# The second block's residual in one flat transfer beside the shifted values, and new order words: a two-stage sequence kernel on one core

## What is computed

```
x = x + _layernorm(_L0_attn_ref(_layernorm(x, axis=-1), ...), axis=-1)
x = x + _layernorm(_L0_ffn_ref(_layernorm(x, axis=-1), ...), axis=-1)
```

```
da = jnp.exp(dt_t[:, :, None] * a)
dbu = dt_t[:, :, None] * b_t[:, None, :] * u_t[:, :, None]
state = da * state + dbu
y_t = jnp.einsum('bds,bs->bd', state, c_t)
```

## Time and profile before

| | us |
|---|---|
| median of 3 runs | 2424.35 |
| lowest and highest run | 2414.93, 2427.51 |
| the profiled execution | 2425.17 |
| its span, first to last instruction | 2423.4 |
| one sequence in the steady state | 136.93 to 139.19 |
| PE, DVE, ACT, POOL busy in the span | 1934.9, 1914.2, 1741.6, 1716.1 |
| the four loads of the residual, each | 64 KB, 2.7 to landing |

### The profile page before, as it was taken

How to read it: one execution, slowest core, us unless ns; L and a number is a source line. 1 busy time by engine, 2 the same in 40 slices (tenths; PEclk the granted TensorE clock), 3 DMA queues, 4 the chain that set the end, 5 groups by cost and what they waited for, 6 DMA issues and landing times.

```text
span 2423.4 us, 43963 instructions
## 1 busy us (share of the span) xinstructions
PE 1934.9 (80%) x15823; PEld 1138.6 (47%) x15936; DVE 1914.2 (79%) x3509; ACT 1741.6 (72%) x3891; POOL 1716.1 (71%) x1572
## 2 busy tenths in 40 slices
PE   2255889798988979797988979797988979788866
PEld 0012446363635446363645546363644536364634
DVE  3557797979889797988888797988889797987442
ACT  2245778696978778696877879696877869686644
POOL 1959596877959596886959596895959597792110
PEclk9967999998999999899999989999999999899988
DMA  5444343535345453535434353534434353541000
GB/s 167 126 114 119 107 119 96 131 101 145 100 118 131 107 123 89 142 82 151 113 110 122 108 125 95 142 91 132 124 105 119 106 133 94 140 104 34 17 16 14
DMA packets 126346, 261.09 MB, mean 108 GB/s; under 512 B 26928, under 2 KB 59696, under 8 KB 125872
## 3 DMA queue, kind: packets, MB, share of 16 engines
q1 hardware_dynamic: 126128, 258.27, 40.4%
HBM read 185.42 MB, written 42.99 MB: 94 GB/s over the span
## 4 chain that ended last, share of the span: by engine, by line
PE 37%; ACT 18%; DVE 18%; POOL 14%; issue 10%; DMA 2%; SPq 0%; POOLq 0%; DVEq 0%; ACTq 0%
POOL dbu L663 5%; POOL gy L680 5%; ACT late L893 4%; DVE m L928 4%; PE b_bank L357 3%; PE f_bank L357 3%; ACT da L609 3%; DVE kr L942 3%; PE b_bank L763 2%; POOL kr L997 2%; PE y_sum L584 2%; PE b_bank L780 2%; PE b_bank L746 2%; PE f_bank L746 2%; PE f_bank L763 2%
## 5 line engine op out<-in xcount | busy, mean ns | idle before, releaser
L629 DVE TENSOR_TENSOR_SCAN hs<-da,dbu 128x512 f32<-128x512 f32 x512 | 623.3, 1217 | 112.5 <-POOL dbu L663 67.6
L680 POOL TENSOR_TENSOR gy<-hs,bc 128x512 f32<-128x512 f32 x512 | 652.7, 1275 | 34.2 <-DVE hs L629 21.8
L663 POOL TENSOR_TENSOR dbu<-spread,bc 128x512 f32<-128x512 f32 x512 | 652.2, 1274 | 16.5 <-DMA spread<-steps 16.5
L609 ACT ACTIVATE da<-spread,rest 128x512 f32<-128x512 f32 x512 | 362.3, 708 | 140.2 <-DVE hs L629 121.1
L720 PE MATMUL b_bank<-rest,h_t 128*128 128x512 f32 x384 | 245.8, 743 | 75.4 <-DVE kr L942 71.5
L997 POOL TENSOR_TENSOR kr<-kr,rn 128x512 f32<-128x512 f32 x256 | 261.0, 1044 | 32.9 <-ACT rn L853 18.4
L720 PE MATMUL f_bank<-rest,h_t 128*128 128x512 f32 x384 | 235.8, 717 | 40.2 <-DVE kr L942 30.4
L584 PE MATMUL y_sum<-gy,rest 128*32 128x512 f32 x1024 | 146.4, 647 | 93.3 <-POOL gy L680 93.3
L357 PE MATMUL b_bank<-first,kr 128*128 128x128 f32 x768 | 127.5, 291 | 82.3 <-DVE kr L942 60.4
L893 ACT ACTIVATE late<-b_bank,mx 128x128 f32<-128x128 f32 x512 | 141.0, 383 | 60.5 <-DVE mx L958 60.5
L1146 POOL TENSOR_TENSOR xs<-xs,v 128x512 f32<-128x512 f32 x16 | 18.9, 1183 | 215.9 <-ACT xs L352 215.9
(11 more groups left out here) (171 smaller groups left out, 4789.3 us busy)
## 6 DMA issues: line engine op xcount, KB each, us to landing
spread<-steps SPq DMA_DIRECT2D x256, 512.0 KB, 4.7
vs<-v SPq DMA_DIRECT2D x96, 260.0 KB, 5.6
steps<-k_t SPq DMA_DIRECT2D x32, 512.0 KB, 3.0
bc<-bc_rows SPq DMA_DIRECT2D x32, 512.0 KB, 6.4
gate<-gates SPq DMA_DIRECT2D x32, 512.0 KB, 5.4
gates<-kr SPq DMA_DIRECT2D x16, 512.0 KB, 2.9
gates<-late SPq DMA_DIRECT2D x16, 512.0 KB, 3.9
vs<-v SPq DMA_DIRECT2D x32, 130.0 KB, 4.7
```

Source lines behind the costliest of these rows:

```text
L609: e.activation(da[:, :], spread[:, slot(b, s // 2), 0, :], ACT.Exp, scale=a_neg[:, s:s + 1]).then_inc(decayed.sem, 1)
L629: e.tensor_tensor_scan(hs[:, s % 2, :], da[:, :], dbu[:, s % 2, :], 0.0, ALU.mult, ALU.add).then_inc(scanned.sem, 1)
L663: e.tensor_tensor(dbu[:, s % 2, :], spread[:, slot(b, s // 2), 1, :], bc[:, s % 2, :], ALU.mult).then_inc(fed.sem, 1)
L680: e.tensor_tensor(gy[:, s % 8, :], hs[:, s % 2, :], bc[:, 2 + s % 2, :], ALU.mult).then_inc(read_out.sem, 1)
```

## The change

- `residual` moves from `wb.v` to `wb.vs[:, 0]`, taken flat as 512 numbers in a row. It lies over the shifted values of the first block, zeroed half included.
- `x1_rows` is laid out by partition (4, P, T) instead of by position, so that the store of x1 and the load of the residual move 2 KB in a row for each partition, and the load is one DMA instead of four. The add on POOL reads flat.
- The wait for `o_made(b - 1)` goes from ACT's first value copy to SP, ahead of the first shifted copy (`sp_windows`, i = 0).
- All five order words are new.

```diff
-        residual = wb.v[:, :, 0:2, 0:DH]
+        residual = wb.vs[:, 0, :, :].rearrange("p h d -> p (h d)")[:, 0:T]
...
-            e.dma_start(x1_rows[b % 4, :, :].rearrange("(t p) d -> p t d", p=P), x1[:, :, :]).then_inc(x1_stored.sem, 16)
+            e.dma_start(x1_rows[b % 4, :, :], x1[:, :, :].rearrange("p t d -> p (t d)")).then_inc(x1_stored.sem, 16)
...
         def sp_windows(E, e, b, w):
             for i in range(2):
+                if i == 0 and w is wb and b > 0:
+                    E.wait_ge(*o_made(b - 1))
                 E.wait_ge(*w.v_copied(b, 2 * i + 1))
...
                 E.wait_ge(*w.projected(b, projections.index(take)))
-                if w is wb and b > 0 and t == 0:
-                    E.wait_ge(*o_made(b - 1))
                 e.activation(w.v[:, t, :, 0:DH], heads(bank_of(take)[:, :]), ACT.Copy).then_inc(w.v_copied.sem, 1)
...
-            x = xs[b % 3][:, :, :].rearrange("p t (g d) -> p t g d", g=2)
+            x = xs[b % 3][:, :, :].rearrange("p t d -> p (t d)")
             E.wait_ge(*o_normed(b))
-            E.wait_ge(*x1_loaded(b, NT - 1))
+            E.wait_ge(*x1_loaded(b))
...
-            for t in range(NT):
-                e.dma_start(residual[:, t, :, :], x1_rows[b % 4, t * P:(t + 1) * P, :].rearrange("p (g d) -> p g d", g=2)).then_inc(
-                    x1_loaded.sem, 16)
+            e.dma_start(residual, x1_rows[b % 4, :, :]).then_inc(x1_loaded.sem, 16)
```

One of the words, SP's, with its delays:

```diff
-        "M3 A1 M8 S2 B1 M1 C1 S1 F2 M9 B1 A1 B1 M1 E1",
-        "A5 B10 C5 E0 F2 M34 S3"),
+        "M4 A1 M4 B2 E1 M1 C1 M2 A1 M3 B1 M5 F1 S2 M1 S1 F1 M2",
+        "A8 B15 C6 E2 F4 M64 S6"),
```

More of the change, by code:

```diff
@@ L43 @@
     "pe": (
[4 rows of a table removed]
[4 rows of a table added]
     "act": (
[5 rows of a table removed]
-    "dve": (
[5 rows of a table removed]
[5 rows of a table added]
+    "dve": (
[5 rows of a table added]
     "pool": (
-        "M5 A1 M1 A2 M12 E1 M31 F4 C1 B2 M1 A1 M3 A1 B1 A1 B1 M4 A1 B2 M2 A2 B1 M3 B2 M2 A1 M3 B3 A2",
-        "A27 B36 C4 E1 F4 M116"),
+        "M3 F4 C1 B1 A1 B1 A2 M2 B1 M2 B1 M1 B1 M2 B1 M1 A1 M2 A1 M1 B1 M1 A1 M2 B1 M1 B1 M2 A1 M1 B3 M1 A1 M2 A1 "
+        "M4 A1 M1 A2 M2 E1 M36",
+        "A24 B36 C4 E0 F4 M70"),
     "sp": (
-        "M3 A1 M8 S2 B1 M1 C1 S1 F2 M9 B1 A1 B1 M1 E1",
-        "A5 B10 C5 E0 F2 M34 S3"),
+        "M4 A1 M4 B2 E1 M1 C1 M2 A1 M3 B1 M5 F1 S2 M1 S1 F1 M2",
+        "A8 B15 C6 E2 F4 M64 S6"),
 }
@@ L269, in build @@
         steps, bc_rows = dram("steps", (2, DI, 2, T)), dram("bc_rows", (2, 2 * NS, T))
-        gates, x1_rows = dram("gates", (2, DI, 2, T)), dram("x1_rows", (4, T, D))
+        gates, x1_rows = dram("gates", (2, DI, 2, T)), dram("x1_rows", (4, P, T))
         x_loaded, e_normed = sig("x_loaded", 1, 16), sig("e_normed", 1)
@@ L293, in build @@
                                                  sig("x2_made", 1))
-        x1_loaded, o_normed, o_made, stored = sig("x1_loaded", NT, 16), sig("o_normed", 1), sig("o_made", 1), sig("stored", 1, 16)
+        x1_loaded, o_normed, o_made, stored = sig("x1_loaded", 1, 16), sig("o_normed", 1), sig("o_made", 1), sig("stored", 1, 16)
         w_loaded, rest_loaded, tables_loaded = sig("w_loaded", 1, 16), sig("rest_loaded", 1, 16), sig("tables_loaded", 1, 16)
```

## The result

| | before | after |
|---|---|---|
| median, us (4 runs each, same chip) | 2419.64 | 2459.68 |
| lowest and highest | 2414.73, 2427.51 | 2457.97, 2459.90 |
| span of the profiled execution | 2423.4 | 2457.9 |

The ratio is 1.016, with a 95% interval of 1.0131 to 1.0188. The forecast was 2420 with a range up to 2444.

The account below looks back on a forecast made before the run. No engine is full, so the period of 137.5 us between residual adds decides. 12.5 periods x -0.5 = -6, plus 2 at the ends, from a profiled 2425.2 lying 0.8 above the median: 2420 us, range 2402 to 2444.

Parts of the forecast that it names:

- The wait off ACT: First value copy's 13.1 us wait for POOL's residual add goes, but ACT's next wait, for POOL's clip, stays: 0.
- The residual's transfer: One load instead of four on SP: the freed 3 us a period stand where nobody waits, 0 to +0.7, taken 0.
- 0.3 to 0.7 us: Cover left before group 12 is read, with the residual's load now ahead of it; POOL would not wait at scan 24.
- The stores: SP's new store order lands the first group about 4 us later, covered by front work: 0 to +2.5, taken 0.
- That leaves 0.5 to 1.5 us: Cover between the first group's later landing and ACT's first da and POOL's first dbu.
- rival (1): Stores pile up beyond the cover, first group 3 us later: +1.8 a period, 2443 us; chance 0.17.
- POOL's work is only exchanged ... By the second and third scan both orders have done the same work: At the first scan, POOL's wait of 0.67 us for the root becomes about 0.8 for the sum of squares.
- rival (2): Reordering shifts PE's pauses and clock: long periods go, 2411, or all become long, 2437; chance of the latter 0.06.
- a mean clock in a period that moves by 0.02: Sign that PE's clock, through the new order, had changed the length of the periods.
- The second step size product: In the entry, later by 1.9 us, of which POOL's work order gives back some 0.6: +1.3.
- The handover: To the next sequence: clip of dt off the chain ahead of `xs`, -0.3 to -0.6 us a period, taken -0.5.
- The ends: First sequence has no cover for du and the loads landing later; last back layer runs alone: +2 us in total.

Follow-up runs that it names:

- code_alone: The changed kernel's code under the five old order words, against the kernel before: 2423.94 us, ratio 0.9992.
- spill_first: The changed kernel with SP storing z, u, x1, b and c ahead of dt and du: 2450.24 us, 1.0106 of the kernel before.
- start_back: spill_first with POOL, ACT and DVE in the old order at the first scan: 2449.62 us, 1.0129 of the kernel before.
- busy_after: The changed kernel with four added products on PE ahead of the back layer's K1 turn: 2444.89 us, 1.0101 of the kernel before.
- busy_more: The kernel before with eight added products in PE's pauses: 2410.56 us, 0.9964 of the kernel before.
- dt_back: spill_first with eight of 24 products of the back layer's last projection behind the second step size product again: 2448.30 us, 1.0118 of the kernel before.
- entry_part: New code, old order, except PE, ACT and DVE in the new order from state norm to handover: 2422.46 us, 1.0015 of the kernel before.
- busy_spill: spill_first plus four added products on PE ahead of the back layer's K1 turn: 2432.00 us, 1.0055 of the kernel before.
- back_first: New code, old order, with the back layer's v3, K1 and k3 ahead of the front's v2 and k2 on PE: 2479.34 us, 1.0241 of the kernel before.

## Why the prediction was wrong, step by step

- **The wait off ACT, 0**: right. In code_alone, which keeps the old order, the 13.1 us of the earlier trace rows are gone and ACT's wait for POOL's `ss` is longer by 15.0. The views of that line, before and in code_alone:

```profile
  POOL ss L988: 56.7, 42
...
  POOL ss L988: 71.7, 42
```

- **The residual's transfer, 0**: right for the transfer itself (code_alone, 0.9992). Its new place is not tested there, since code_alone has the old words, and the "0.3 to 0.7 us" of cover for group 12 was too much. The group issued at 929.46 landed 5.8 us later, at 935.3, and POOL waited for it at scan 24, where I had said that it would not:

```profile
935.33 1.28 POOL L664 TENSOR_TENSOR dbu<-spread,bc 128x512 f32<-128x512 f32 x1 [0.34 <-DMA spread<-steps]
```

  It does so in six of the twelve periods, by 0.2 to 1.2 us, 3.5 in all, where before it was one of 0.5. From the middle gate to the last `gy` a period takes 0.15 us more than before, so this is worth 2 us of the total at most.

- **The stores, 0**: wrong, a term of the sum that was mis-sized. du's landing 7.8 after dt's issue came out (7.9), and the first group is later by 2.8, but the first number is luck: I took the five issues at 2.3 us and the bytes as the brake. The issues themselves take 4.4 us, as SP's rows show, and du's store then lands 3.5 after its issue, not the 5.3 that I gave as a sign. "That leaves 0.5 to 1.5 us" of cover was too much: the group issued at 989.97 landed 5.5 us later, at the very start of the first `da` at 995.51. Nothing was left for the cases in which it is late. This is rival (1), at +0.5% (spill_first) instead of +0.8, and paid elsewhere than I said: 0.3 us a period instead of 1 to 2.5, and the rest at the start and the end.
- **"POOL's work is only exchanged ... By the second and third scan both orders have done the same work"**: this is the step that failed. The first `dbu` comes 1.56 us later (7.20 after the add, before 5.64; I had 2.3), and start_back shows that this does not set the middle gate. But I stopped the comparison at the third scan. The order was new 28 us later too, where the front's v2 and k2 products now stand behind K1: PE idles for 5.0 us and then works at a clock of 0.79, and that costs 1.3 us a period (busy_after). In the two periods above POOL's waits inside the scans went from 2.3 to 4.3 us. Two of them, just behind PE's slow stretch, are the sum of squares from DVE and the root from ACT:

```profile
889.38 0.24 POOL L989 TENSOR_SCALAR ss<-ss 128x16 f32<-128x16 f32 x1 [0.89 <-DVE ss L916]
890.26 1.04 POOL L998 TENSOR_TENSOR kr<-kr,rn 128x512 f32<-128x512 f32 x1 [0.64 <-ACT rn L852]
```

- **PE's clock, rival (2)**: the mechanism was right, the chance was not. "If the later scans give longer pauses, all become long", 2437, had 0.06. They do: PE's pause ahead of K1 is 5.0 us and the middle gate is late in all twelve periods. The sign that I gave for it, a mean clock in a period that moves by 0.02, did not show: it is 0.96 in the period above as in a short one before. I had the long periods' price (2.15) and their clock in the rows, but looked for PE's new pause only at the first scan, where the clock costs at most 0.3 us a period (busy_more). The Trainium skill, "TensorE: Matmul & The Clock Gate", section "What's actually happening", has the clock fall when PE idles; the trace agrees (4.99 us of pause, then 0.79). A walk along the new order would have paid, to every place where PE waits for DVE ahead of products that it could do.
- **The second step size product, +1.3**: near in size (from `x1` to dt it takes 1.6 us more), and without effect on the period: dt_back.
- **The handover, -0.5**: the gain of 6 us in the sum did not come. The clip of dt left the chain ahead of `xs`, but entry_part is at 1.0015 and its mean period at 138.0. From dt to the add it takes 0.8 us less, from `x1` to dt 1.6 more.
- **The ends, +2**: 3.6 at the start and -1.0 at the end, 2.6. The net is near, and what spill_first won at the start (3.8) is of the size of the whole loss there.

What stays open: the 0.55% of busy_spill, some 1 us a period, of which 0.8 lie behind the middle gate. The product and the two DVE steps that now stand ahead of the add are the likely cause; no run tried them alone.

## What to carry to other kernels

Compare two orders of work along the whole period, not only where the diff was explained: find each place where an engine now waits for something behind which it has work that could go ahead, and price it from the longest wait there. Where a kernel has periods of two lengths, take the cause of the longer one as a rival for any reordering: here a new order of five products made all of them long (back_first). The mean clock of a period does not show this: ask where in the period the clock falls, and whether the other engines have a gap there. A few idle products in PE's pauses are a cheap test of whether its clock is the cause, and can be kept if they are faster.

## What the runs showed of the hardware

- An issue on SP is not of fixed length. In spill_first, where dt and du stand apart from the other stores, the six stores take 0.33 to 0.47 us each (medians of the 16 sequences). In the changed kernel, behind two stores of 512 KB issued 0.4 us apart, the next of 512 KB took 0.89 us in the sequence shown, the smaller ones of x1 and of b and c 1.24 and 1.20, and du's 0.77; du's takes at least 0.76 in each of the 16 sequences.

```profile
L395 SPq DMA_DIRECT2D steps<-k_t x16: 757/774/1227, 46.7 to 2109.2; - x16
...
L395 SPq DMA_DIRECT2D steps<-k_t x16: 359/365/365, 47.2 to 2100.2; - x16
```

  The first row is the changed kernel's (min, median, max in ns), the second spill_first's.
- PE's clock falls and rises within one period (0.65, then 0.83 in windows of 6 and 8 us of one whose mean is 0.94), and it matters although PE is idle for 23% of the span: filling one pause of 5 us won 1.3 us a period (busy_after against the changed kernel), with more work on PE.
- 112 more products (busy_more, eight in each of 14 sequences) made the kernel before 0.36% faster.
